# An AdaLN attention and mixture-of-experts kernel: another way to the slot numbers, and a GpSimd normalisation on the mean itself

## The reference, cut to what matters

```
logits = tokens @ gate_w.T                  # 4096 tokens, 16 experts
top1   = argmax(logits)
ranks  = cumsum(one_hot(top1), axis=0) - 1  # how many earlier tokens chose this expert
mask   = one_hot(top1) * (ranks < capacity) # capacity = 320
```

## Time and profile before

| | |
|---|---|
| runs | 217.38 us median of 3 (215.89 to 218.58) |
| profiled execution, span from first to last instruction | 217.0 us |
| what lies around the span in the profiled execution | not given apart; the span is 0.38 us under the median of the runs |
| TensorE (PE) busy | 192.2 us, 89% |
| VectorE (DVE) busy | 153.2 us, 71% |
| ScalarE (ACT) busy | 145.0 us, 67% |
| GpSimd (POOL) busy | 113.8 us, 52% |
| mean granted TensorE clock | 0.967 |

### The profile page before, as it was taken

The page is one execution under the profiler, slowest core; times in us unless marked ns, Lnnn a source line. Parts: engine busy times, 40 slices in busy tenths (PEclk is TensorE's granted clock), DMA queues, the critical chain, the costliest instruction groups (busy, mean ns, idle before and its releaser), DMA issues.

```text
span 217.0 us, 4034 instructions
## 1 busy us (share of the span) xinstructions
PE 192.2 (89%) x1177; PEld 155.3 (72%) x1177; DVE 153.2 (71%) x476; ACT 145.0 (67%) x425; POOL 113.8 (52%) x139
## 2 busy tenths in 40 slices
PE   6999599999999979999988749999999999999930
PEld 4789377788879759775665414888878889788830
DVE  3657999999999999999996407156847668485430
ACT  4494868999999979987756641574855848555300
POOL 6311504431387828577767760002754378487774
PEclk9788999999999999999999996999999999999996
DMA  5999999507905013114453216999879585321000
GB/s 149 285 343 360 355 360 309 222 5 215 270 21 177 0 53 147 48 73 138 161 186 119 99 65 159 362 358 357 277 254 283 168 268 157 85 100 46 31 30 20
DMA packets 37284, 38.60 MB, mean 178 GB/s; under 512 B 2591, under 2 KB 31334, under 8 KB 37264
## 3 DMA queue, kind: packets, MB, share of 16 engines
q1 hardware_dynamic: 33936, 31.29, 46.1%
q0 software_dynamic: 3328, 7.07, 9.1%
HBM read 19.19 MB, written 18.95 MB: 176 GB/s over the span
## 4 chain that ended last, share of the span: by engine, by line
PE 59%; DVE 17%; issue 8%; POOL 7%; ACT 4%; DMA 2%; POOLq 1%; SPq 0%; DVEq 0%
PE bank L1280 14%; PE bank L1266 11%; PE bank L1039 5%; POOL out_dram L529 4%; PE bank L1083 3%; PE bank L1109 3%; PE bank L1057 3%; PE bank L1092 2%; PE bank L1078 2%; PE bank L1094 2%; PE bank L1050 2%; DVE kvsum L780 2%; PE bank L1327 2%; PE bank L1237 2%; DVE rows L804 2%
## 5 line engine op out<-in xcount | busy, mean ns | idle before, releaser
L529 POOL DMA_INDIRECT out_dram<-x_all,rest x40 | 43.2, 1080 | 42.2 <-DVE x_all L985 23.8
L503 POOL DMA_INDIRECT dispatched_rows<-rows,slot x32 | 32.2, 1006 | 16.0 <-issue 9.0
L709 ACT ACTIVATE HT<-bank 128x320 f32<-128x320 f32 x64 | 28.0, 438 | 10.2 <-PE bank L1266 9.8
L1280 PE MATMUL bank<-HT,w 128*128 128x320 f32 x112 | 32.4, 432 | 0.0
L1280 PEld LDWEIGHTS bank<-HT,w 128*128 128x128 f32 x112 | 20.6, 189 | 6.7
L1266 PE MATMUL bank<-xth,w1h 128*128 128x320 f32 x64 | 22.6, 353 | 0.2 <-DVE xtl L961 0.2
L955 DVE TENSOR_TENSOR w1l<-w,w1h 128x1024 fp32r<-128x1024 f32 x8 | 16.1, 2022 | 7.4 <-DMA dispatched_rows<-rows,slot 7.4
L1004 DVE COPY OT<-bank 128x320 f32<-128x320 f32 x14 | 6.9, 492 | 18.5 <-PE bank L1280 18.5
L1266 PE MATMUL bank<-xth,w1l 128*128 128x320 f32 x64 | 19.8, 309 | 0.0
L1266 PE MATMUL bank<-xtl,w1h 128*128 128x320 f32 x64 | 19.8, 309 | 0.0
L560 ACT ACTIVATE junk<-bank 128x128 f32<-128x128 f32 x64 | 16.5, 288 | 1.5 <-PE bank L1039 1.3
(11 more groups left out here) (172 smaller groups left out, 494.1 us busy)
## 6 DMA issues: line engine op xcount, KB each, us to landing
w<-in_L_ffn_w_dram SPq DMA_DIRECT2D x16, 512.0 KB, 7.6
dispatched_rows<-blank SPq DMA_DIRECT2D x8, 965.0 KB, 13.2
rest<-dispatched_rows SPq DMA_DIRECT2D x8, 645.0 KB, 6.4
hin<-dispatched_rows SPq DMA_DIRECT2D x7, 320.0 KB, 7.5
x_all<-in_L_attn_x_dram SPq DMA_DIRECT2D x8, 256.0 KB, 5.2
rows<-gb_row SPq DMA_DIRECT2D x8, 256.0 KB, 3.8
out_dram<-rows SPq DMA_DIRECT2D x8, 256.0 KB, 3.2
out_dram<-x_all,rest POOLq DMA_INDIRECT x40, 2.3
```

The costliest lines, as they stand in the source:

```text
L503: pool.indirect_dma_start(out=disp_d, out_offset=bass.IndirectOffsetOnAxis(ap=slot[:, b, j:j + 1], axis=0), in_=rows[:, b, j, :], in_offse ...
L529: pool.indirect_dma_start(out=out_d.rearrange("b t d -> (b t) d"), out_offset=bass.IndirectOffsetOnAxis(ap=rest[i % RING][:, n, C_TOK - D: ...
L709: act.activation(HT[e][:, f, :], ps_h[c % HB][:, 0:CAP], ACT.Gelu_apprx_tanh).then_inc(h_done, 1)
L1280: last = pe.matmul(ps_o[e], w2[i % RING][:, e, f, :], HT[e][:, f, :], start=(f == 0), stop=(f == NF - 1))
```

## The change

The count of a token's rank is made to start at its expert's first slot. `seen` no longer starts at zero: its first tile holds `expert * 320 / 128` in each of the 128 partitions, so that the sum over partitions adds `expert * 320`. The triangle loses its diagonal, so that a token doesn't count itself. What TensorE sums is then the row number itself. `slots` compares it with `limit` (`(expert + 1) * 320`), adds 1 << 20 where it is over, multiplies with the one-hot tile and sums over the experts into whole numbers: four operations, each waiting for the one before. `claim` of bank `t` now waits for the second of them (`place_done`).

GpSimd's `normalize1` uses the mean and `rs1` as VectorE's does, and `shift1` with its semaphore goes: 7 operations less on VectorE. GpSimd's start gets two small operations more and a subtraction in place of a cast.

```diff
--- before.py
+++ after.py
@@ -127,7 +127,6 @@
         mv1 = sb("mv1", [P, NJ, 2])
         ln1 = sb("ln1", [P, NJ])
         rs1 = sb("rs1", [P, NJ])
-        nm1 = sb("nm1", [P, NJ])
         xh = sb("xh", [P, NJ, D])
         NHT = 5
         hT = [sb(f"hT{n}", [P, T]) for n in range(NHT)]
@@ -189,9 +188,9 @@
         oh = [sb(f"oh{n}", [P, NJ, NE], bf16) for n in range(2)]
         seen = sb("seen", [P, NJ, NE], bf16)
         rk = sb("rk", [P, NJ, NE])
-        rank = sb("rank", [P, NJ])
-        sl_a = sb("sl_a", [P, NJ])
-        sl_o = sb("sl_o", [P, NJ])
+        over = sb("over", [P, NJ, NE])
+        place = sb("place", [P, NJ, NE])
+        limit = sb("limit", [P, NJ, NE])
         slot = sb("slot", [P, NB, NJ], i32)
 
 
@@ -226,15 +225,16 @@
              "GT_done")]
         (x1_ps, x1_done, ln2_st, ln2_mv, ln2_ln, ln2_rs, nm2_done, xh2_done, xh2T_ps, h2T_done, h2_ps,
          h2_done, logit_ps, mx_done, dl_done, pe_done, psm_done, prob_done, cand_done, best_done,
-         oh_done, seen_done, rank_ps, rk_done, rank_done, sl_done, slot_done,
+         oh_done, seen_done, rank_ps, rk_done, over_done, place_done, slot_done,
          gb_in) = [sem(n) for n in (
              "x1_ps", "x1_done", "ln2_st", "ln2_mv", "ln2_ln", "ln2_rs", "nm2_done", "xh2_done", "xh2T_ps",
              "h2T_done", "h2_ps", "h2_done", "logit_ps", "mx_done", "dl_done", "pe_done",
              "psm_done", "prob_done", "cand_done", "best_done", "oh_done",
-             "seen_done", "rank_ps", "rk_done", "rank_done", "sl_done", "slot_done", "gb_in")]
+             "seen_done", "rank_ps", "rk_done", "over_done", "place_done", "slot_done", "gb_in")]
         pool_past = sem("pool_past")
+        limit_done = sem("limit_done")
         last_sent = sem("last_sent")
-        ek_done, shift1_done = sem("ek_done"), sem("shift1_done")
+        ek_done = sem("ek_done")
         w1h_done, w1l_done, xth_done = sem("w1h_done"), sem("w1l_done"), sem("xth_done")
         x1_out, scattered = sem("x1_out"), sem("scattered")
         w1_in = [sem(f"w1_in{n}") for n in range(RING)]
@@ -287,15 +287,9 @@
 
             after(eng, ln1_rs, b)
             after(eng, xhT_ps, b, 1)
-            if eng is nc.gpsimd:
-                eng.wait_ge(shift1_done, b)
             for j in range(NJ):
-                if eng is nc.gpsimd:
-                    last = eng.tensor_scalar(xh[:, j, :], x_all[:, b, j, :], rs1[:, j:j + 1],
-                                             nm1[:, j:j + 1], ALU.mult, ALU.add)
-                else:
-                    last = eng.tensor_scalar(xh[:, j, :], x_all[:, b, j, :], mv1[:, j, 0:1],
-                                             rs1[:, j:j + 1], ALU.subtract, ALU.mult)
+                last = eng.tensor_scalar(xh[:, j, :], x_all[:, b, j, :], mv1[:, j, 0:1],
+                                         rs1[:, j:j + 1], ALU.subtract, ALU.mult)
             last.then_inc(xh_done, 1)
 
         def modulate1(eng, b):
@@ -461,7 +455,7 @@
             pool.memset(ident[:, :], 0.0).then_inc(pool_setup, 1)
             pool.memset(blank[:, :], 0.0).then_inc(pool_setup, 1)
             pool.memset(ones_b[:, :], 1.0).then_inc(pool_setup, 1)
-            pool.memset(seen[:, :, :], 0.0).then_inc(pool_setup, 1)
+            pool.memset(seen[:, 1:NJ, :], 0.0).then_inc(pool_setup, 1)
             pool.iota(rev_i[:, :], pattern=[[0, NJ], [-1, NE]], base=NE, channel_multiplier=0
                       ).then_inc(pool_setup, 1)
             pool.iota(tokid[:, :], pattern=[[P, NTOK // P]], base=0, channel_multiplier=1
@@ -473,11 +467,14 @@
             pool.affine_select(out=tri[:, 0:P], in_=tri[:, 0:P], compare_op=ALU.is_ge, fill=0.0,
                                base=0, pattern=[[1, P]], channel_multiplier=-1).then_inc(consts, 1)
             pool.wait_ge(consts, 2)
-            pool.tensor_copy(tri_b[:, :], tri[:, 0:P]).then_inc(consts, 1)
+            pool.tensor_tensor(tri_b[:, :], tri[:, 0:P], ident[:, :], ALU.subtract).then_inc(consts, 1)
             rows_t = rows[:, :, :, :].rearrange("p b j c -> p (b j) c")
             pool.tensor_copy(rows_t[:, :, C_TOK].bitcast(i32), tokid[:, :])
             pool.tensor_copy(rev[:, :, :].rearrange("p j e -> p (j e)"), rev_i[:, :]).then_inc(consts, 1)
+            pool.tensor_scalar(seen[:, 0, :], rev_i[:, 0:NE], -CAP / P, NE * CAP / P, ALU.mult, ALU.add)
             pool.memset(ones[:, :], 1.0).then_inc(ones_done, 1)
+            pool.tensor_scalar(limit[:, :, :].rearrange("p j e -> p (j e)"), rev_i[:, :], -float(CAP),
+                               float((NE + 1) * CAP), ALU.mult, ALU.add).then_inc(limit_done, 1)
 
             def squares(b):
                 after(pool, hT_done, b)
@@ -732,13 +729,6 @@
                     last = dve.bn_aggr(mv1[:, j, :], st1[:, j, :])
                 last.then_inc(ln1_mv, 1)
 
-            def shift1(b):
-
-                after(dve, ln1_rs, b)
-                after(dve, xh_done, b, 1)
-                dve.scalar_tensor_tensor(nm1[:, :], mv1[:, :, 0], -1.0, rs1[:, :], ALU.mult, ALU.mult
-                                         ).then_inc(shift1_done, 1)
-
             def h_means(b):
                 after(dve, mh_ps, b)
                 after(dve, nrl_done, b, 1)
@@ -857,19 +847,19 @@
                 dve.reciprocal(rows[:, b, :, C_PROB], psm[:, :]).then_inc(prob_done, 1)
 
             def slots(b):
+                if b == 0:
+                    dve.wait_ge(limit_done, 1)
                 after(dve, rank_ps, b)
-                dve.tensor_tensor(rk[:, :, :], oh[b % 2][:, :, :],
-                                  ps_rank.rearrange("p (j e) -> p j e", e=NE), ALU.mult
-                                  ).then_inc(rk_done, 1)
+                ranked = ps_rank.rearrange("p (j e) -> p j e", e=NE)
+                dve.tensor_tensor(over[:, :, :], ranked, limit[:, :, :], ALU.is_ge).then_inc(over_done, 1)
+                dve.wait_ge(over_done, b + 1)
+                dve.scalar_tensor_tensor(place[:, :, :], over[:, :, :], float(NOWHERE), ranked, ALU.mult, ALU.add
+                                         ).then_inc(place_done, 1)
+                dve.wait_ge(place_done, b + 1)
+                dve.tensor_tensor(rk[:, :, :], place[:, :, :], oh[b % 2][:, :, :], ALU.mult).then_inc(rk_done, 1)
                 dve.wait_ge(rk_done, b + 1)
-                dve.tensor_reduce(rank[:, :], rk[:, :, :], X, ALU.add).then_inc(rank_done, 1)
-                dve.wait_ge(rank_done, b + 1)
-                dve.scalar_tensor_tensor(sl_a[:, :], best[:, b, :], -float(CAP), rank[:, :], ALU.mult, ALU.add)
-                dve.tensor_scalar(sl_o[:, :], rank[:, :], float(CAP), float(NOWHERE), ALU.is_gt, ALU.mult
-                                  ).then_inc(sl_done, 1)
-                dve.wait_ge(sl_done, b + 1)
-                dve.scalar_tensor_tensor(slot[:, b, :], sl_a[:, :], float(NE * CAP - 1), sl_o[:, :],
-                                         ALU.add, ALU.add).then_inc(slot_done, 1)
+                with nc.allow_low_precision(reason="one term of the sum is a whole number, the others are 0"):
+                    dve.tensor_reduce(slot[:, b, :], rk[:, :, :], X, ALU.add).then_inc(slot_done, 1)
 
             dve.memset(eps[:, 0:1], EPS_LN)
             dve.memset(eps[:, 1:2], 1e-06)
@@ -923,20 +913,20 @@
 
             dve.wait_ge(consts, 4)
 
-            stats1(1); aggregate1(1); shift1(1); stats1(2); h_means(0); aggregate1(2); qk_means(0)
-            stats1(3); modulations(); scan_w(0); weigh_v(0); denominator(0); shift1(2)
+            stats1(1); aggregate1(1); stats1(2); h_means(0); aggregate1(2); qk_means(0)
+            stats1(3); modulations(); scan_w(0); weigh_v(0); denominator(0); 
             normalize1(dve, 2); scan_kv(0); h_means(1); qk_means(1); modulate1(dve, 2); diagonal(0); aggregate1(3)
-            stats1(4); weigh_v(1); diagonal(1); clamp_g(0); shift1(3); normalize1(dve, 3); scan_w(1)
+            stats1(4); weigh_v(1); diagonal(1); clamp_g(0); normalize1(dve, 3); scan_w(1)
             denominator(1); h_means(2); gate_u(0); aggregate1(4); stats1(5); scan_kv(1); residual(0)
-            qk_means(2); shift1(4); weigh_sums(dve, 1); h_means(3); stats2(0); aggregate2(0)
+            qk_means(2); weigh_sums(dve, 1); h_means(3); stats2(0); aggregate2(0)
             clamp_g(1); scan_w(2); modulate1(dve, 4); weigh_v(2); aggregate1(5); shift2(0); stats1(6)
-            silu(dve, 1); gate_u(1); qk_means(3); denominator(2); h_means(4); shift1(5)
+            silu(dve, 1); gate_u(1); qk_means(3); denominator(2); h_means(4); 
             normalize2(dve, 0); scan_kv(2); residual(1); scan_w(3); weigh_sums(dve, 2)
             modulate1(dve, 5); denominator(3); weigh_v(3); qk_means(4); clamp_g(2); stats2(1)
             h_means(5); scan_kv(3); top_value(0); top_expert(0); top_prob(0); aggregate1(6); stats1(7)
-            aggregate2(1); scan_w(4); shift2(1); shift1(6); gate_u(2); slots(0); qk_means(5)
```

(7 more changed lines are left out.)

## The result

The changed kernel takes 220.42 us, the median of 20 runs (219.03 to 222.27); beside it on the same chip the kernel before takes 218.19 (20 runs, 215.89 to 219.68). The ratio is 1.0135 [1.0106, 1.0164]: slower by 1.35%, some 2.9 us, where 0.8 us less was forecast. It lies within the 2% that the chances spoke of, but above the range. Ratios here leave out runs more than 1.5% above their kernel's fastest, so one can differ from the quotient of two medians.

A forecast was written before the change was run, and what follows sets the result against it. Bound by full TensorE, VectorE and ScalarE from 35 to 60 us, GpSimd's products near 71 us, and VectorE's list from b=5's slots to the last scatter. Terms: -0.4 - 0.1 + 0.1 - 0.5 + 0.1 = -0.8, giving 216.6 us, range 214.7 to 218.4.

The forecast's parts named there:

- The subtraction in GpSimd's normalising: GpSimd's normalising: subtracting first reads as many operands as the multiply did, so it was counted as 0.
- the bound of +1.7: Upper bound in us at b=7, should subtracting first double the time of GpSimd's normalising block.
- early enough: GpSimd's normalising at b=1: no gain counted from dropping its wait for VectorE's product.
- a full TensorE: At b=4 and 5 GpSimd's normalising can start earlier, but TensorE's list behind it is full: no gain counted.
- The block of b=7 earlier, -0.4: GpSimd's normalising at b=7 starts without waiting for VectorE's product: -0.4 us, bounds 0 and -0.47.
- Seven products less, -0.1: VectorE without its seven products: -0.1 us for one or two on its chain, bounds 0 and -0.5.
- The slots, +0.1 and -0.5 at b=5: VectorE's new slots: +0.1 us for dearer operations, -0.5 us at b=5 because GpSimd disturbs them less.
- Bank t: TensorE's next user of the bank waits for the slots' second operation, 0.25 us later: counted as 0.
- the start: GpSimd's added setup, at most 0.6 us, stands before 4.32 us of idle time: counted as 0.
- collisions: Earlier GpSimd normalising meets VectorE's two-input products: +0.1 us at b=4; as a rival, 218.3 us, chance 0.14.
- the dear subtraction: Rival: subtracting first is dear on GpSimd, +1.7 us at b=7 through the chain, 219.1 us; chance 0.03.
- The case of all gains through: Rival: slots undisturbed, gains at their bounds and the +0.1s away, 215.6 us; chance 0.10.

The follow-up runs named there:

- experiment 3: Changed kernel with other operation pairs in GpSimd's normalising tiles, output not the reference's; one execution: 0.45 us for (mult, add), 0.79 to 0.82 for pairs with a subtract.
- experiment 1: Kernel before with only the new normalising (subtract, mult; the seven VectorE products gone), old slots kept: 221.46 us, ratio 1.0127 to the kernel before.
- experiment 7: Changed kernel normalising as (x + (-mean)) * rs1; mean negated on VectorE: 217.45 us, 0.9972 to the kernel before; negated on GpSimd: 216.35 us, 0.9936.
- experiment 6: New slots with the old normalising, the subtraction form at one place only; ratios to the kernel before: b=1 1.0032, b=4 and 5 1.0018, b=6 1.0011.
- experiment 2: Changed kernel with the old normalising and the seven products put back, so only the new slots stay: 217.10 us, 0.9957 to the kernel before.
- 4: Changed kernel with b=7 alone normalised by the old product form, VectorE's product for b=7 back: 219.92 us, 1.0104 to the kernel before.
- the second of 7: Changed kernel normalising as (x + (-mean)) * rs1, with GpSimd itself negating the mean: 216.35 us, 0.9936 to the kernel before.
- its repeat: The changed kernel run again, unaltered, beside other runs on the same chip: 1.0107 to the kernel before, shortest span 217.3 us.
- 5: Changed kernel with the old product form back at b=1, 4 and 5, the subtraction left at b=6 and 7: 218.91 us, 1.0027 to the kernel before.
- the first of 7: Changed kernel normalising as (x + (-mean)) * rs1, with VectorE negating the mean: 217.45 us, 0.9972 to the kernel before.
- experiment 8: Changed kernel with a useless VectorE memset of 512 columns ahead of top_value(1), to shift when cand is asked for: 220.95 us, 1.0153 to the kernel before.

## Why the prediction was wrong, step by step

**The step that failed** is "The subtraction in GpSimd's normalising": "It reads as many operands as the multiply did ... I take 0". The operands are the same and the time is not: 0.45 us a tile became 0.80 (experiment 3), 9.1 us of GpSimd became 16.3. By itself this edit costs about 2.8 us (experiment 1), and with the pair changed to (add, mult) and the edit else kept the loss is gone (experiment 7). The chance of 0.03 rested on "nothing speaks for it but the missing row". A missing row is no evidence for zero; the bound of +1.7 stood in the text with too little weight, and it was too low, because it was laid on b=7 alone. b=1, dismissed as "early enough", does delay VectorE by 0.87 us, by a wait for the end of the block that was in the code (aggregate1 may not overwrite the means before xh is done), though only 0.22 us of it is left at gs. b=4 and 5, where a full TensorE was the reason for counting nothing on the earlier start, are 0.58 us at gs, and b=6, which the bound didn't price, is 0.8 of the 2.77 us there (experiment 6).

**The block of b=7 earlier, -0.4.** Right and overrun: it starts with no idle time but ends 1.41 - 0.47 = 0.94 us later against the squares ahead of it (gs starts at 72.38 against 71.35, while those squares start at 68.23 against 68.12).

**Seven products less, -0.1.** Small, as taken; nothing in the experiments separates it from zero. Experiment 7 has a negation where the product was, and lies within experiment 2's interval.

**The slots, +0.1 and -0.5 at b=5.** Right. Each new operation takes 0.22 to 0.23 us, the list goes on after 0.91 us at b=5. (The shortest 4-column operation of the earlier trace rows is L739 with 151 ns, not 160; nothing hangs on it.) The sum of these two terms is -0.4; experiment 2 measured about -0.9 [-1.7, -0.1].

**Bank t, the start, collisions.** The view of the line L856 names nobody who waited for place, TensorE included. GpSimd is idle for 3.48 us ahead of its squares at 8.40, against 4.32: the new setup is hidden. At b=4 it was GpSimd that was stretched (3.66 us instead of 3.14), not VectorE's yT: 0.68 us, as in the earlier trace rows.

**The rivals.** It was the dear subtraction that came true, in kind, at about 2.8 us for that edit alone (experiment 1) instead of 1.7. Its own test was in the prediction: "wrong if L294's pieces are longer than 0.45 us". (The case of all gains through was mis-added: 217.38 - 0.47 - 0.6 - 0.5 is 215.8, not 215.6; the range doesn't hang on it.) The other row that the prediction had pointed to, the stretched operations at 72 to 74 us, is real and grew to 4.07 us, but the loudest row of the profile was not where most of the time went. cand held is 4 us of VectorE, yet GT for b=3, which waits for gs but not for that yT (it is b=4's), was late before too, behind three held operations. Counted from the start of gs, GT began 4.07 to 4.10 us later in the seven profiles with the long hold and 3.44 to 3.46 in the seven without, so the hold costs GT 0.64 us. TensorE waits as well, for the one-hot tile that follows cand, which it didn't before:

```profile
76.52 0.20 PE L1118 MATMUL bank<-oh,tri_b 128*128 128x64 bf16 x1 [1.64 <-DVE oh L838]
```

The kernel without the hold and with b=7 short (4) is faster by 0.3 to 0.7 us, within the wide interval given there.

## What to carry to other kernels

An operation that an engine has not been seen doing has no price, even when operands, shape and buffers stay the same: time the exact pair of operations first, or keep the pair and change the data (here the sign of the mean). When an instruction grows, look through the code for all who wait for its end, buffer waits of the early stages included, and then follow in the trace how much of the delay the next waits swallow: of 0.87 us at b=1 a quarter was left later. Two single profiles whose clock fell at different places can hide a change of 1.3%, which the ratio of many runs shows. For parts of it, a few tenths of a us each, whole times were too coarse and ranked the places differently by each measure, while the distance between two steps of one trace repeated within 0.04 us.

## What the runs showed of the hardware

**GpSimd's price by pair.** On 128x128 f32 tiles 0.45, 0.61 or 0.80 us by the operations alone (experiment 3). VectorE does (subtract, mult) on tiles of the same shape in 0.34 us (b=2 and 3, L291 of the changed kernel).

**A hold over several instructions.** Where cand beside b=7 began 0.62 to 0.64 us before the end of GpSimd's running instruction, it was through shortly after that end: 0.70 to 0.72 us, in seven profiles (the kernel before, experiments 2, 4, the three of 6, the second of 7). Where it began 0.22 to 0.52 us before that end, it was held until GpSimd's whole row of back-to-back work was through: 2.55 to 4.07 us, in seven others (the changed kernel and its repeat, experiments 1, 3, 5, 8, the first of 7). The first of 7 shows that it isn't the long tiles: cand began at 71.72 beside gs, which ended at 70.68 + 1.28 = 71.96.

```profile
71.72 2.55 DVE L844 SCALAR_TENSOR_TENSOR cand<-dl,rev 128x64 f32<-128x64 f32 x1
```

```profile
70.68 1.28 POOL L286 TENSOR_TENSOR gs<-gc,sg 128x512 f32<-128x512 f32 x1
71.93 1.26 POOL L279 TENSOR_TENSOR yT<-kvsum,rden 128x512 f32<-128x512 f32 x1
73.16 1.03 POOL L490 TENSOR_TENSOR hsq<-hT 128x512 f32<-128x512 f32 x1
```

The Trainium skill (SBUF — State Buffer, "Who interferes with whom") says that the one which comes first holds the shared ports for its whole instruction. The 0.70 us of the earlier trace rows agree with that; these rows go beyond it, since cand got no turn when gs ended at 71.96 nor when yT ended. What decides between the two was not found: in these profiles the moment at which cand begins goes with the outcome, but that it is the cause is not shown, since the only attempt (experiment 8) missed the place.
